# Reordering the start of a two-layer transformer kernel: modulation weights first, small inputs on a second queue, query weights split later

## What is computed

```
# layer 0
proj = cond @ W_ada.T + b_ada;  scale, shift = proj[:, :C], proj[:, C:]
h = layernorm(x) * (1 + scale) + shift
q = h @ Wq.T;  c_kv = h @ Wkd.T;  k = c_kv @ Wku.T;  v = c_kv @ Wvu.T
x = x + softmax(mask(rope(q) @ rope(k).T)) @ v @ Wo.T
# layer 1
h = rmsnorm(x) * ln1_w * (1 + cond @ tw1.T)
x = x + attention(h; rope by pos_ids) @ Wo.T
h = rmsnorm(x) * ln2_w * (1 + cond @ tw2.T)
x = x + (silu(h @ Wg.T) * (h @ Wu.T)) @ Wd.T
```

## Time and profile before

| | |
|---|---|
| median of 3 runs | 1775.21 us |
| the profiled execution's own time | 1777.36 us |
| its span, first to last instruction | 1775.6 us |
| PE busy | 1705.9 us, 96% |
| DVE / ACT / POOL busy | 1149.6 / 944.0 / 396.4 us |
| mean granted PE clock | 0.982 |

### The profile page before, as it was taken

The page is one execution under the profiler, slowest core; times in us unless marked ns, Lnnn a source line. Parts: engine busy times, 40 slices in busy tenths (PEclk is TensorE's granted clock), DMA queues, the critical chain, the costliest instruction groups (busy, mean ns, idle before and its releaser), DMA issues.

```text
span 1775.6 us, 37783 instructions
## 1 busy us (share of the span) xinstructions
PE 1705.9 (96%) x12440; PEld 930.8 (52%) x12440; DVE 1149.6 (65%) x2858; ACT 944.0 (53%) x2769; POOL 396.4 (22%) x556
## 2 busy tenths in 40 slices
PE   6676999999999999999999999999999999999999
PEld 2344545555555555555455555555555554555444
DVE  6758666676768667685676766686676856767320
ACT  3836466354755538464573547555384645735320
POOL 3438496021111011111110211110111111102120
PEclk9788999999999999999999999999999999999999
DMA  7876499353876449571793638763485817935310
GB/s 246 151 192 119 129 236 246 90 100 99 179 150 112 92 115 192 113 137 55 164 185 87 103 98 177 152 113 90 115 193 114 137 56 169 190 84 98 109 64 24
DMA packets 527227, 234.24 MB, mean 132 GB/s; under 512 B 476336, under 2 KB 493744, under 8 KB 527024
## 3 DMA queue, kind: packets, MB, share of 16 engines
q1 hardware_dynamic: 511472, 175.09, 49.6%
q10 hardware_dynamic: 15552, 56.63, 10.3%
HBM read 90.09 MB, written 16.78 MB: 60 GB/s over the span
## 4 chain that ended last, share of the span: by engine, by line
PE 75%; DMA 3%; DVE 3%; POOL 2%; issue 2%; ACT 1%; SPq 0%; DVEq 0%; ACTq 0%; POOLq 0%
PE up L1451 8%; PE up L1453 8%; PE up L1452 8%; PE gate L1451 8%; PE gate L1453 8%; PE gate L1452 8%; PE y L1453 4%; PE y L1451 4%; PE y L1452 4%; PE bank L1451 3%; PE bank L1453 3%; PE bank L1452 3%; DMA prob_t<-prob 2%; PE bank L1478 2%; PE bank L1486 1%
## 5 line engine op out<-in xcount | busy, mean ns | idle before, releaser
L879 ACT ACTIVATE bank<-bank,low 128x128 f32<-128x128 f32 (+2 forms) x768 | 302.5, 395 | 66.2 <-DVE low L1121 33.2
L704 POOL TENSOR_TENSOR inner_t<-inner,inner_t 128x512 f16<-128x512 f32 x128 | 150.9, 1179 | 640.0 <-ACT inner_t L1060 640.0
L1128 DVE TENSOR_TENSOR prob<-bank,prob 128x512 f16<-128x512 f32 (+1 forms) x320 | 202.8, 634 | 53.6 <-ACT prob L888 52.7
L888 ACT ACTIVATE prob<-bank 128x512 f16<-128x512 f32 (+1 forms) x320 | 178.3, 557 | 72.8 <-DMA prob_t<-prob 44.5
L1406 DVE SCALAR_TENSOR_TENSOR silu<-silu,gate 128x512 f32<-128x512 f32 x128 | 87.9, 686 | 170.9 <-ACT silu L1054 170.1
L1451 PE MATMUL gate<-mlp,ring 128*128 128x512 f16 x512 | 193.9, 379 | 1.6 <-DVE silu L1406 1.4
L1451 PE MATMUL up<-mlp,ring 128*128 128x512 f16 x512 | 193.8, 379 | 0.4 <-DVE inner L1416 0.4
L1453 PE MATMUL gate<-mlp,ring 128*128 128x512 f16 x512 | 194.0, 379 | 0.0
L1452 PE MATMUL gate<-mlp,ring 128*128 128x512 f16 x512 | 193.9, 379 | 0.0
L1453 PE MATMUL up<-mlp,ring 128*128 128x512 f16 x512 | 193.9, 379 | 0.0
L1452 PE MATMUL up<-mlp,ring 128*128 128x512 f16 x512 | 193.9, 379 | 0.0
(11 more groups left out here) (182 smaller groups left out, 4021.7 us busy)
## 6 DMA issues: line engine op xcount, KB each, us to landing
ring<-wgu_dram ACTq DMA_DIRECT2D x108, 512.0 KB, 3.9
x_in<-x_dram SPq DMA_DIRECT2D x18, 512.0 KB, 3.9
x_res<-x_mid SPq DMA_DIRECT2D x16, 512.0 KB, 3.1
wgu_dram<-ring SPq DMA_DIRECT2D x16, 512.0 KB, 3.6
out_dram<-x_res SPq DMA_DIRECT2D x32, 256.0 KB, 2.2
prob_t<-prob SPq DMA_TRANSPOSE x256, 3.5
inner_t<-wd_t_dram SPq DMA_DIRECT2D x4, 1024.0 KB, 9.3
ring<-wg_t_dram SPq DMA_DIRECT2D x16, 256.0 KB, 4.2
```

The lines of the kernel that those rows point to most:

```text
L704: pool.tensor_tensor(inner_t[:, 1, f, :], inner[:], inner_t[:, 0, f, :], ALU.subtract).then_inc(inner_low, 1)
L879: ins = act.activation(bank_[:, at:at + wid], bank_[:, at:at + wid], ACT.Exp, bias=low[:, j % BANKS, k:k + 1], scale=-1.0, accum_out=total)
L888: act.activation(terms(prob[:, g % SLOTS, 0, :], layer, j), terms(work_bank[USE[f"unit{layer}", j] % BANKS][:], layer, j), ACT.Copy).then_ ...
L1128: dve.tensor_tensor(terms(prob[:, slot, 1, :], layer, j), terms(work_bank[USE[name] % BANKS][:], layer, j), terms(prob[:, slot, 0, :], lay ...
```

## The change

- SP issues `ada0`, `ada1`, both sequences of `x_in`, then `kv` and `wq0` as before. The four small inputs (`cond`, `pos`, `freq`, `b_ada`) are issued from ACT's queue, as its first instructions.
- PE first multiplies the identity by itself ten times into bank `y1`, which nothing reads.
- DVE takes `mod_copies(0)` ahead of the first statistics, and `ln_apply` of sequence 0 ahead of `mod_copies(1)`, and `ln_apply` of sequence 1 behind the gains.
- ACT makes the high halves of all six pieces before it modulates the first tokens; before, the four of `wq0` came after that.
- DVE makes the low halves of `wq0` two pieces ahead of the values of sequence 0 and two ahead of those of sequence 1 (`kv.0`, `kv.1`); before, all four came ahead of the latent's low half (`lat.0`).

```diff
-PIECES_AT = {"first": range(0, 2), "lat.0": range(2, 6), "unit0_9": range(6, 7), ...
+PIECES_AT = {"first": range(0, 2), "kv.0": range(2, 4), "kv.1": range(4, 6), "unit0_9": range(6, 7), ...
 # SP
-            load_x((None, 0), 0)
-            sp.dma_start(cond, cond_t.rearrange("(c p) s -> p c s", p=P)).then_inc(cond_in, 16)
-            sp.dma_start(b_ada[:], b_ada_t).then_inc(cond_in, 16)
-            load_pos((None, 0))
-            sp.dma_start(freq[:], freq_c).then_inc(freq_in, 16)
             load("ada0")
             load("ada1")
+            load_x((None, 0), 0)
             load_x((None, 0), 1)
 # ACT
-            def weight_highs(step):
-                for piece in PIECES_AT.get(step, ()):
-                    if piece >= DVE_PIECES:
-                        continue
+            def weight_highs():
+                for piece in range(DVE_PIECES):
                     act.wait_ge(*landed[PIECE_OF[piece][0]])
...
+            act.dma_start(cond, cond_t.rearrange("(c p) s -> p c s", p=P)).then_inc(cond_in, 16)
+            act.dma_start(pos[:], pos_dram[0]).then_inc(pos_in, 16)
+            act.dma_start(freq[:], freq_c).then_inc(freq_in, 16)
+            act.dma_start(b_ada[:], b_ada_t).then_inc(cond_in, 16)
             sines_((None, 0))
-            weight_highs("first")
+            weight_highs()
 # DVE
+            mod_copies(0)
             ln_stats((None, 0), 0)
-            mod_copies(0)
             ln_stats((None, 0), 1)
+            ln_apply((None, 0), 0)
             mod_copies(1)
-            for s in BOTH:
-                ln_apply((None, 0), s)
             gains(0)
+            ln_apply((None, 0), 1)
             weight_lows("first")
 # PE
+            pe.wait_ge(ident_made, 1)
+            for _ in range(10):
+                pe.matmul(ybank[1][:, 0:P], ident[:], ident[:], start=True, stop=True)
             pe.wait_ge(cond_in, 32)
             for k in range(2):
                 for c in range(CH):
                     conditioning(k, c)
-            pe.wait_ge(ident_made, 1)
```

More of the change, by code:

```diff
@@ L158 @@
 PIECE, DVE_PIECES = 512, 6
-PIECES_AT = {"first": range(0, 2), "lat.0": range(2, 6), "unit0_9": range(6, 7), "unit0_11": range(7, 8),
+PIECES_AT = {"first": range(0, 2), "kv.0": range(2, 4), "kv.1": range(4, 6), "unit0_9": range(6, 7), "unit0_11": range(7, 8),
              "unit0_14": range(8, 9), "unit0_16": range(9, 10), "unit0_18": range(10, 11)}
@@ L895, in ahead @@
                         tanhs(m, chunks_at(m, step, 2))
-                    else:
-                        weight_highs(step)
-                        if step == "fill2.0":
-                            act.wait_ge(gains_made, 4 * CH)
+                    elif step == "fill2.0":
+                        act.wait_ge(gains_made, 4 * CH)
                     if step == SINES_AT:
```

## The result

The changed kernel took 1779.74 us in the median of its 14 runs, the kernel before 1775.74 beside it; the ratio is 1.0022 (95% interval 1.0015 to 1.003). One of the 14 took 5399.59 us and is left out of the ratio. A second series of the same kernel gave 1777.14 us and 1.0016 (1.0007 to 1.0025). Forecast was 1772.1, in a range up to 1774.5, with a chance of 0.03 for slower. Both the sign and the range were wrong.

What follows compares the result with a forecast made beforehand. SP's queue, its start set by the keys, was taken to bound the first scores; minus 3.65 plus 0.5 plus 0.1 gave minus 3.05, say 3.1 us, so the median goes from 1775.21 to 1772.1, range 1769.9 to 1774.5.

Steps and rivals of the forecast that it cites:

- Loads: Modulation weights issued first at the head: `ada0` lands about 7.1 us, 2.5 us earlier issued; `wq0` gains about 0.9, landing 16.8.
- Small inputs on ACT's queue: At the head, `freq` is issued at 1.7 us from ACT and lands at 4.9; ACT itself loses nothing.
- a rival at 0.17: Small inputs starve beside the full stream at the head: `freq` near 8, DVE's cast 21.6, total 1773.6 us; chance 0.17.
- Identities: Ten products in PE's idle head raise its clock, so `ada0`'s products end at 14.3 us, not 16.6; worth at most 0.7.
- The gains, and ACT's weights first: Before the first modulation: gains ready 6.2 us earlier, at 16.5, but `wq0` and its high halves bind; modulation starts 3.65 earlier.
- Query lows beside the values: On DVE, second `v_lo` starts at 34.2, not 33.69: 0.5 us lost on the keys' path, 1.5 on the queries'.
- the cover of 0.6 us on the query path: Ahead of SP's transposes, queries stacked at 41.0 and keys done at 41.6, so the queries' loss was covered by 0.6 us.
- PE's clock in the queries: PE idles about 3 us ahead of the queries; restarting at the lower clock costs 0 to 2.3 us, taken as 0.1.
- slower: PE falls to the lower clock for all 48 query products, 10.3 us more, total 1782.6 us; chance 0.03.
- The lead moves as a whole: After the first scores, all that follows in the first pair waits by semaphores and moves with them, keeping the 3.1 us.
- absorbed: Later first-pair work (POOL's weight splitting, DMA landings, the clock) takes up the lead: no change, 1775.2 us; chance 0.08.
- Sum: Over the first pair's head: minus 3.65, plus 0.5, plus 0.1, giving minus 3.05, say 3.1 us.

Runs made afterwards that it cites:

- the best version: The changed kernel with the four small inputs issued by SP ahead of the modulation weights and without the ten identity products: 0.9986, 1772.58 us; again 0.9986, 1773.7 us.

## Why the prediction was wrong, step by step

*Loads.* Right in kind: the hole is closed. `ada0` was to land at 7.1; PE's first product on it came at 8.01 where nothing else held it (small inputs by SP, whose four issues put `ada0`'s to 2.74). `wq0` was to land at 16.8; the high halves began at 16.89, and at 17.52 and 17.43 in the two kernels where the trace names `wq0` as what they waited for.

*Small inputs on ACT's queue.* **This step failed.** `freq` was to land at 4.9 after "the 3.2 us of today"; POOL began on it at 8.52. I had this as a rival at 0.17, `freq` near 8, cast at 21.6; the cast came at 23.12, since `b_ada`, last in the queue, also held PE, which I hadn't listed (PE waits for `cond` and `b_ada` by one semaphore). The Trainium skill (DMA: Bandwidth & Descriptors, Queues, rings and completion order) says that an engine takes its queues in turn, one packet from each; the 930 packets of q10 beside 996 of q1 agree with it. I named that rule and gave the case it describes too small a chance. Two series that differ in this part alone put its price at 0.0015 (2.7 us) with identities. Without identities it is 0.0013 (2.3 us), from series taken apart and hardly clear of their intervals, and the traces don't bear it out at the head: the first scores come at 48.49 us in both.

*Identities.* **This step failed, and it set the sign.** The text priced them as "worth at most 0.7 us" and gave them no cost, because they lie in idle time. In the change PE stood 3.16 us for `b_ada` behind them, and its granted clock was at the lower level from 10.0 us on for 3.4 us: the eight products took 5.30 us against 5.94 before and 5.00 in the change without identities. (The 1.00 that the earlier trace rows print for the granted clock in 7 to 12 us is no measured level: the trace's first record of it is at 14.4 us, and the spacing of the products, 0.85 us ahead of it and 0.43 behind it, tells the level, as the prediction read it.) With the small inputs in time they were worth more than 0.7 at the head: `up` took 4.96 us with ten and 6.16 and 6.54 without, the first scores 47.12 against 48.49 and 49.31. And they cost 2.95 us in all (1777.14 less 1774.19), by the place of the code behind them, a cost that no list of waits of the kernel before contains. No rival held it either.

*The gains, and ACT's weights first.* "`wq0` is the new bound" was wrong for this kernel, since the biases were later (21.39 instead of 19.1), and right where the small inputs come in time and the identities stand ahead: 19.73, released by the high halves. There the first scores came at 47.12; forecast was 46.2 or so. Without the identities ACT waits 1.31 and 1.58 us for DVE's biases again (20.93 and 21.30), since `up` takes longer.

*Query lows beside the values.* The 0.5 us lost on the keys' path can't be seen in the times: two pairs of series with and without the move differ by 0.0003 and 0.0001, with intervals of 0.001 to either side. But the cover of 0.6 us on the query path was a misjudgement: the keys were done at 44.08 and SP issued the queries only at 44.49. The last of their stacked copies ended at 45.37 on ACT, as against 43.16. The query path was the later one.

*PE's clock in the queries.* PE's first query products, between 34 and 37.3 us, took 0.43 us apart and the later ones 0.215. This is the price between 0 and 2.3 that I had set at 0.1; it is about 1.65 us (eight gaps between starts took 3.37 us in place of 1.72). The granted clock was 0.50 between 34 and 37.3 us and 0.99 before and after, and PE had stood 2.72 us for `wq_lo` until 33.25. The "slower" rival had this mechanism for all 48, and was wrong.

*The lead moves as a whole.* **This step failed too.** The prediction let all that follows the first scores move with them. With the lead there (2.2 us at the first scores), 2.0 us were left at 137.2 us and 0.5 at 182.8, and the series came to 1.0001. Without it (0.04 and 0.86 us at the first scores) the two series came to 0.9986. What the stretch between 137 and 183 us does, minus 2.2 or plus 1.5 us, is as large as the forecast and doesn't follow the head. Of the rivals, *absorbed* came nearest to this, with a chance of 0.08 and the argument that each step starts on a semaphore.

*Sum.* 0.9986 for the version without the two failed parts is 2.5 us, near the 3.1 forecast. That is luck: the 3.1 were to be had at the first scores, and there this version has 0.9 and 0.0. The parts add up (0.9986, plus 0.0015 for the small inputs, plus 0.0017 for the identities, is 1.0018, between the change's two series of 1.0016 and 1.0022), but the times add up and not the mechanism of the forecast.

## What stays open

That the place of PE's code decides over the loss is shown by runs (one column against full, behind the loop against ahead, 64 against 25). How it does so is only argued. The pieces of 16 KB are fetched at other moments, and the probabilities' transposes, which run at the same DMA engines, land later: their median in the kernels with 0, 10 and 25 full products is 3.5, 3.6 and 3.8 us. No run moved the fetches alone. Nor is the first pair settled: the kernel before has none ahead of its loop, as the best version has, and yet it shows 0.83 and 0.72 for the stretches at 166 and 178 us. So there the place is one of at least two things that decide, and the 2.2 us that the versions without products gain on the kernel before between 137 and 183 us isn't explained by their heads. Since it is there that the best version gets ahead in both its traces, what its 0.9986 comes from is open, too.

## What to carry to other kernels

Work that fills an engine's idle time isn't free when it moves the code behind it: ten products cost 3 us here, and no less with one column; twenty-five cost 12, and 22 with one column. Put it in as one-column products first, and see whether the time behind it moves, before crediting or blaming the work. And follow a lead to the end of its stretch, not only to the first scores. Small inputs on a second queue beside a full stream moved at that stream's pace, packet for packet (930 beside 996); let them go first on one queue and the large loads behind them (four issues, 1775.56 against 1777.14 us here). And when a change has a part that "can only help", run the kernel without it: here the version without two such parts was faster than both kernels, twice (0.9986), if not for the forecast reason.

## What the runs showed of the hardware

- The instruction queue moved 13 or 14 pieces of 16 KB in each pass of the loop, about 207 us, so the loop's code was loaded again in every pass. One more piece in the pass went with jumps back of 2.05 to 3.75 us instead of 0.40 to 0.45.
- A shift by 40 instructions of the same engine doubled a wait on another engine (ACT for transposed probabilities, 19.5 to 47.4 us over 1.1 ms); one by 256 left it near that (26.0).
- Float32 products of the identity with one column lasted as long as the first ones with 128: 10, 25 and 64 of one column took 4.4, 10.8 and 27.5 us, 0.43 each; ten full ones took 4.6. Of 25 full ones, 8.2 us in all, those until 6.4 us stood 0.43 apart and the later ones 0.22.
- The eight `up` products took 3.61 us behind 25 full products, and 6.14 and 5.87 behind 25 and 64 of one column, though these had started 0.43 us apart right up to them.
- Small rows on a second queue took 5.7 to 6.9 us to land beside the full stream, and 1.7 to 2.4 us as the first issues of the only queue.
